# A decoder layer with self-attention, cross-attention and a ternary feed-forward: the projections of cross-attention spread over all units, and all eight key blocks by high and low parts

## The reference

```
x = x + attn(layernorm(x))        # 16 heads of 128, window of 128 keys, rope, sink
x = x + xattn(layernorm(x), ctx)  # below
x = x + ffn(layernorm(x))         # 8-bit rows, ternary weights, Hadamard transform

Q = (query @ Wq).reshape(b, q_len, G, Hpg, dh)       # 512 rows, 16 heads of 32
K = (key @ Wk).reshape(b, kv_len, G, dh)             # 1024 keys, 4 groups of 32
V = (value @ Wv).reshape(b, kv_len, G, dh)
scores = einsum('bqghd,bkgd->bghqk', Q, K) / sqrt(dh) + m * rel
w = softmax(where(mask, scores, neg), axis=-1)
out = einsum('bghqk,bkgd->bqghd', w, V).reshape(b, q_len, G * Hpg * dh) @ Wo
```

## Time and profile before

| | |
|---|---|
| median of three runs | 1842.2 us (1842.17 to 1844.28) |
| profiled execution, its own time | 1846.15 us |
| span from first to last instruction in it | 1844.3 us |
| busy: PE, DVE, ACT, POOL | 1667.3, 1161.6, 1238.9, 1176.8 us |
| mean granted clock of PE | 0.973 |

### The profile page before, as it was taken

How to read it: one execution, slowest core, us unless ns; L and a number is a source line. 1 busy time by engine, 2 the same in 40 slices (tenths; PEclk the granted TensorE clock), 3 DMA queues, 4 the chain that set the end, 5 groups by cost and what they waited for, 6 DMA issues and landing times. The chain is left out here.

```text
span 1844.3 us, 24894 instructions
## 1 busy us (share of the span) xinstructions
PE 1667.3 (90%) x8112; PEld 1164.3 (63%) x8112; DVE 1161.6 (63%) x2031; ACT 1238.9 (67%) x2018; POOL 1176.8 (64%) x1080
## 2 busy tenths in 40 slices
PE   6999979899999957999999999999999966999996
PEld 3588868788888845556655565556555523666664
DVE  2378868677666743666675558655776724677763
ACT  2366768787656631797777678766886924878775
POOL 0477857678778810566665557555675727888892
PEclk9999989999999988999999999999999988999999
DMA  6222343333000012311211122011011211011000
GB/s 218 103 66 85 98 127 109 92 115 127 13 18 7 29 42 67 107 40 36 72 46 49 35 75 61 12 38 44 18 43 41 97 58 64 13 35 35 24 18 23
DMA packets 57647, 110.76 MB, mean 60 GB/s; under 512 B 9132, under 2 KB 13996, under 8 KB 57136
## 3 DMA queue, kind: packets, MB, share of 16 engines
q1 hardware_dynamic: 55680, 108.04, 18.8%
q10 hardware_dynamic: 1840, 1.14, 0.2%
HBM read 71.33 MB, written 18.88 MB: 49 GB/s over the span
## 5 line engine op out<-in xcount | busy, mean ns | idle before, releaser
L1263 POOL TENSOR_TENSOR x_p_lo<-x_p,x_p_hi 128x1024 fp32r<-128x1024 f32 x192 | 455.7, 2385 | 300.6 <-ACT x_p_hi L1097 300.1
L1212 DVE TENSOR_REDUCE x_maxes<-x_ps_a 128x1 f32<-128x1024 f32 x256 | 313.1, 1223 | 258.5 <-PE x_ps_a L1346 257.6
L1075 ACT ACTIVATE x_p<-x_ps_b,x_any_valid 128x1024 f32<-128x1024 f32 x256 | 285.1, 1114 | 168.7 <-PE x_ps_b L1334 167.9
L1334 PE MATMUL x_ps_b<-x_Q,x_K 100*128 100x512 f32 x512 | 228.3, 527 | 3.7 <-ACT x_p L1075 2.2
L1097 ACT ACTIVATE x_p_hi<-x_p 128x1024 fp32r<-128x1024 f32 x192 | 203.1, 1058 | 4.8
L1346 PE MATMUL x_ps_a<-x_K,x_Q 99*128 99x512 f32 x512 | 166.8, 407 | 6.4 <-DMA x_Q<-x_p_lo 3.7
L1372 PE MATMUL x_ps_o<-x_p_hi,x_V 128*96 128x512 f32 x384 | 157.2, 409 | 1.1 <-POOL x_p_lo L1263 1.1
L1334 PEld LDWEIGHTS x_ps_b<-x_Q,x_K 100*128 100x128 f32 x512 | 90.1, 190 | 97.2 <-issue 76.2
L1373 PE MATMUL x_ps_o<-x_p_lo,x_V 128*96 128x512 f32 x384 | 150.9, 393 | 0.0
L427 ACT ACTIVATE a_work<-a_ps_s,a_neg_max,a_q_r 128x256 f32<-128x256 f32 (+1 forms) x256 | 134.1, 540 | 4.6 <-DVE a_neg_max L527 4.6
L619 POOL TENSOR_TENSOR a_work<-a_work,a_inv_den 128x1024 f32<-128x1024 f32 (+1 forms) x64 | 110.0, 1719 | 18.6 <-DVE a_inv_den L567 18.6
(11 more groups left out here) (243 smaller groups left out, 4315.4 us busy)
## 6 DMA issues: line engine op xcount, KB each, us to landing
shared<-in_L_attn_out_w SPq DMA_DIRECT2D x8, 1024.0 KB, 7.7
shared<-in_L_ffn_w_gate SPq DMA_DIRECT2D x16, 512.0 KB, 4.5
shared<-in_L_ffn_w_up SPq DMA_DIRECT2D x16, 512.0 KB, 4.1
shared<-in_L_ffn_w_down SPq DMA_DIRECT2D x16, 512.0 KB, 4.1
shared<-in_ctx SPq DMA_DIRECT2D x8, 1024.0 KB, 7.0
x_Q<-x_q_hi SPq DMA_DIRECT2D x104, 64.0 KB, 2.0
ffn_quant<-shared SPq DMA_DIRECT2D x24, 256.0 KB, 4.6
a_xt<-in_x SPq DMA_DIRECT2D x16, 256.0 KB, 4.9
```

Source lines behind the costliest of these rows:

```text
L1075: act.activation(p[:, r, :, :], ps_b[:, :, :], ACT.Exp, scale=any_valid[:, b % 2:b % 2 + 1]).then_inc(exp_ready, 1)
L1212: dve.tensor_reduce(out=maxes[:, h2, r, 3:4], in_=ps_a[:, :, :], axis=mybir.AxisListType.XY, op=ALU.max)\
L1263: pool.tensor_tensor(out=p_lo[:, r], in0=p[:, r], in1=p_hi[:, r].bitcast(F32), op=ALU.subtract).then_inc(lo_ready, 1)
L1334: last = pe.matmul(ps_b[:, j, :], K[0:ROWS + 4, g, kb * P:(kb + 1) * P], Q[0:ROWS + 4, hh, :], start=True, stop=True)
```

## The change

In cross-attention:

- All four units of a head now go by high and low parts. `V32` and the plain fp32 matmuls are gone, `V` holds all eight key blocks, ACT makes `p_hi` and POOL `p_lo` in every unit. `p` is a ring of three (was four, one to each r), `p_hi` of four (was three), `p_lo` stays at three, each with the waits that belong to it. `aT` has five slots instead of four.
- The jobs are no longer bound to heads. A table `ORDER` of twelve jobs gives job n of a batch the units 5n to 5n + 3, so that every fifth unit has none. Part 2 of Q is now made in the batch that uses it. The transposed norm goes through `ps_x` (units r = 3 of heads 2 to 5), not through `ps_j`.
- The prologue projects keys before it transposes the norm, makes two parts of Q instead of three, and copies the constant key rows later.
- The last output projection runs over the head groups outside and the four tiles inside, into four banks.

In self-attention the rounding of weights moves two steps later, and the exchange of sums is split into `store_sums` (steps 9, 17, 25) and `load_sums` (steps 11, 19, 27). In the feed-forward phase the first two tiles are loaded already during cross-attention, and the constants are waited for later.

```diff
-            def exchange_sums(t):
+            def store_sums(t):
                 sp.wait_ge(f_sum_ready, t + 1)
                 sp.dma_start(ffn_total[t:t + 1, :].rearrange("a p -> p a"), f_sum[:, t:t + 1]).then_inc(f_sum_out, 16)
+
+            def load_sums(t):
                 sp.wait_ge(f_sum_out, 16 * (t + 1))
                 sp.dma_start(f_all[:, t, :], ffn_total[t:t + 1, :].broadcast_to([P, P])).then_inc(f_all_in, 16)
...
-                if 0 <= c - 16 < FFN_CHUNKS:
-                    store_quant(c - 16)
-                if 0 <= c - 12 < FFN_CHUNKS:
-                    load_raw(c - 12)
+                if 0 <= c - 18 < FFN_CHUNKS:
+                    store_quant(c - 18)
+                if 0 <= c - 14 < FFN_CHUNKS:
+                    load_raw(c - 14)
                 if c in (9, 17, 25):
-                    exchange_sums(c // 8 - 1)
+                    store_sums(c // 8 - 1)
+                if c in (11, 19, 27):
+                    load_sums(c // 8 - 1)
...
-        V = sb("V", [P, 2, 6, GX, 3 * DH], F32R)
-        V32 = sb("V32", [P, 2, 2, GX, 3 * DH])
+        V = sb("V", [P, 2, KB, GX, 3 * DH], F32R)
         maxes = sb("maxes", [P, HX, TPB, 4])
-        p = sb("p", [P, 4, 2, T])
-        p_hi = sb("p_hi", [P, 3, 2, T], F32R)
+        p = sb("p", [P, 3, 2, T])
+        p_hi = sb("p_hi", [P, 4, 2, T], F32R)
         p_lo = sb("p_lo", [P, 3, 2, T], F32R)
...
+        ORDER = (("Q", 2, 0), ("Q", 3, 0), ("K", 0, 1), ("K", 1, 1), ("out", 0, -1), ("out", 1, -1), ("out", 2, -1), ("out", 3, -1),
+                 ("Q", 0, 1), ("V", 0, 1), ("V", 1, 1), ("Q", 1, 1))
+        pieces, finished, finished_at = {}, [], {}
+        for b in range(-1, B):
+            jobs = [(8 * b + 4 * (n - 9), (name, i, 0)) for n, (name, i, later) in enumerate(ORDER) if name == "V"] if b < 0 else \
+                [(4 * HX * b + 5 * n, (name, i, b + later)) for n, (name, i, later) in enumerate(ORDER) if 0 <= b + later < B]
...
-                    if c and r < 3:
-                        act.wait_ge(lo_ready, 3 * (c - 1) + r + 1)
-                    if c and r == 3:
-                        act.wait_ge(pv_done, 4 * c)
-                    act.activation(p[:, r, :, :], ps_b[:, :, :], ACT.Exp, scale=any_valid[:, b % 2:b % 2 + 1]).then_inc(exp_ready, 1)
+                    if v >= 3:
+                        act.wait_ge(lo_ready, v - 2)
+                    act.activation(p[:, v % 3, :, :], ps_b[:, :, :], ACT.Exp, scale=any_valid[:, b % 2:b % 2 + 1]).then_inc(exp_ready, 1)
...
-                if 0 <= c < HEADS and r < 3:
-                    pool.wait_ge(hi_ready, 3 * c + r + 1)
-                    if c:
-                        pool.wait_ge(pv_done, v - 3)
-                    pool.tensor_tensor(out=p_lo[:, r], in0=p[:, r], in1=p_hi[:, r].bitcast(F32), op=ALU.subtract).then_inc(lo_ready, 1)
+                if 0 <= c < HEADS:
+                    pool.wait_ge(hi_ready, v + 1)
+                    if v >= 3:
+                        pool.wait_ge(pv_done, v - 2)
+                    else:
+                        pool.wait_ge(q_spread[1], 192)
+                    pool.tensor_tensor(out=p_lo[:, v % 3], in0=p[:, v % 3], in1=p_hi[:, r].bitcast(F32), op=ALU.subtract).then_inc(lo_ready, 1)
...
-                    if rw < 3:
-                        pe.wait_ge(lo_ready, 3 * kw + rw + 1)
-                        for j in range(2):
-                            vs = V[:, bw % 2, 2 * rw + j, gw, :]
-                            pe.matmul(bank[0:ROWS, :], vs, p_hi[:, rw, j], start=(rw == 0 and j == 0), stop=False)
-                            last = pe.matmul(bank[0:ROWS, :], vs, p_lo[:, rw, j], start=False, stop=False)
-                    else:
-                        pe.wait_ge(exp_ready, w + 1)
-                        for j in range(2):
-                            last = pe.matmul(bank[0:ROWS, :], V32[:, bw % 2, j, gw, :], p[:, 3, j], start=False, stop=(j == 1))
+                    pe.wait_ge(lo_ready, w + 1)
+                    for j in range(2):
+                        vs = V[:, bw % 2, 2 * rw + j, gw, :]
+                        pe.matmul(bank[0:ROWS, :], vs, p_hi[:, rw, j], start=(rw == 0 and j == 0), stop=False)
+                        last = pe.matmul(bank[0:ROWS, :], vs, p_lo[:, w % 3, j], start=False, stop=(rw == 3 and j == 1))
...
+            for k in range(GX):
+                G = GX * (B - 1) + k
+                pe.wait_ge(aT_ready, G + 1)
+                for i in range(TPB):
+                    last = pe.matmul(banks[i], aT[:, G % (GX + 1), i * P:(i + 1) * P], wo_sb[:, k, :], start=(k == 0), stop=(k == GX - 1))
+                    if k == GX - 1:
+                        last.then_inc(job_made, 1)
```

260 lines of the change are left out of this document (127 added, 133 removed).

## The result

The kernel after takes 1790.3 us (median of four runs, 1788.45 to 1790.5) against 1842.2 us for the kernel before in the same session: a ratio of 0.971 (95% interval 0.970 to 0.973), faster by 2.9%. The forecast was 1786 us. The profiled execution took 1788.45 us for a span of 1786.2; for it the sum of the prediction gave about 1790.

The account below looks back on a forecast made before the run. PE was taken as the bound, narrowly in free heads. Terms -30 - 14 - 2 - 5 - 5 = -56 us took the profiled 1846.15 us to about 1790; the median, 4 us lower, gave 1786 us, 8-in-10 range 1765 to 1808.

Parts of the forecast that it names:

- Units of cross-attention: Cross-attention stage: two middle batches -14.0 us each, first batch -7, last +4.5; together -30 us, bounds -50 and -10.
- The step on the output projection: First output piece waits for aT behind p_lo; ACT partly catches up, leaving 3 to 3.5 us, three times.
- The step on free units: Around job-free units in cross-attention, late exponentials make PE wait 6 to 7 us a batch, 1.5 more at its end.
- rival 1: Cross-attention: PE stays the bound throughout; batch 176 us, stage -50, whole 1766 us; chance 0.20.
- The plain matmuls go: Cross-attention: replacing plain fp32 matmuls saves PE 0.78 us a head, 12.5 a batch, 50 us over 64 heads.
- the spreading: Cross-attention: with a unit between jobs, PE's hand-over waits at ps_j go, most of 12.2 us in a batch.
- Free heads: Cross-attention heads without a job: bound by POOL and ACT at about 9.76 us, 9.27 before.
- Self-attention: Weight rounding: ACT's waits of 9.8 and 6.4 us for a stored chunk go; -14 us, bounds -18 and 0.
- feed-forward: Start of the feed-forward phase: rows in place, only memsets ahead of layer norm; -5 us, bounds -5 and -1.
- Rival 2: Cross-attention: ACT and POOL hold PE up in every head; stage -8 us, whole 1808 us; chance 0.22.
- rival 4: Cross-attention: VectorE slows p_lo on POOL; at 3.2 us each the kernel takes about 1870 us; chance 0.04.
- Rival 3: Self-attention: the wait only moves, the store landing late instead of being issued late; whole 1800 us; chance 0.09.

Follow-up runs that it names:

- e1: Kernel after, with POOL making aT ahead of p_lo instead of behind it in units r = 3; 1773.5 us.
- e9: Kernel after, with four useless plain fp32 matmuls filling PE's wait for aT at the first piece of the output projection; 1785.6 us.
- e5: Kernel before, with only the high and low parts for all eight key blocks, jobs still bound to heads; 1869.9 us.
- e6: Kernel after, with the last two key blocks of a head in plain fp32 and the old rings, new job order kept; 1787.4 us.
- e7: Kernel after with aT made ahead of p_lo, and ACT's copy into den moved to DVE; 1777.7 us.
- e3: Kernel after, with self-attention's weight rounding and exchange of sums as in the kernel before; 1800.4 us.

## Why the prediction was right, and where it was not

The total was right by 4 us. A part of this is luck. The spans of the two profiled executions differ by 58.1 us (1844.3 to 1786.2) where the sum had 56, but the medians by 51.9: the prediction took 4 us off because the kernel before was profiled in an execution 4 us above its median, and the kernel after was profiled in one 2 us below its own. The parts, by the two spans:

- **Units of cross-attention: -33.9 for -30.** The middle batch was 184.3 for 185.3, the first 9.6 us shorter for 7, the last 15 heads 6.3 longer for 4.5. The agreement in the middle batch is luck: errors that cancel. The step on the output projection, "ACT catches up its own lateness meanwhile, so I count 3 to 3.5 us, three times", failed: the wait itself was sized well (4.04 for 4.4), but it was not made good, and the clock, for which the sum has no term, fell behind it. e1 takes away 5.4 us at each place and leaves a wait of 1.2, e9 puts 2.6 of the 5.4 to the clock. So this place costs 3.4 us more than the 3.2 of the sum, and the low clock of head 46 another 1.6. The step on free units, "6 to 7 us in a batch, with 1.5 us more", was too high by 4: there are 3.3 us of waits for exponentials in a middle batch, 1.7 of them in the four free units at its end and 1.6 in all others. And PE's own work is 172.75 us at the full clock (e1) where the sum had 174.6. Together +3.4, +1.6, -4.2 and -1.9 make the 1 us between forecast and trace. With aT out of the way the batch is 177.2 us, so away from that one place rival 1 (176 us) describes the kernel better than the forecast does.
- **"The plain matmuls go ... 50 us over 64 heads".** The size per head was exact where PE is the bound (13.36 to 12.58), but the term is no gain of its own. Alone it made the kernel 28 us slower (e5); with the jobs spread and aT first it is worth 14 us (e6 against e1). What carried the change is the spreading: 37.6 us over the 63 heads without the high and low parts. The prediction took 12.2 us of waits out of a middle batch and put 10.7 us of new ones in, so that spreading had 1.5 of its 14 us; by e6 it is 13.4 us in that batch (199.0 to 185.6).
- **Free heads: 9.78 for 9.76.** Right; which engine sets it was left as "POOL and ACT". e7 shows ACT first: with one copy less on ACT the head is 9.36 us, all of it POOL's work.
- **Self-attention: -13.3 for -14** in the two profiled spans, but -9.5 to -10 by e3 and the means over all traces. The two spans flatter this term by 3 to 4 us. The step took the waits as nearly gone ("no wait on the stored chunk above 2 us"); waits of 2.8 and 3.4 us are left.
- **Prologue -3.2 for -2, end of cross-attention -4.6 for -5, feed-forward -3.1 for -5.** The first two are sizes: the prologue lasts 38.0 to 38.6 us in the eleven traces with its code. The last failed in its step "only the memsets are ahead": the layer norm does start at once, but POOL's `f_ln_rstd` comes 4.9 us into the phase, and the identity lands 8.5 us after its issue. So the term is not there at all: the 3.1 us are what two traces happen to differ by, and the means over all traces are 0.3 us apart (326.5 and 326.2).
- **Rival 2** (PE held in every head, 7.2 us in units with a piece) is refuted by 3.3 us of waits for exponentials in the whole of a middle batch, **rival 4** by p_lo, which stayed at 2.34 to 2.44 us in all 256. **Rival 3** (the wait in self-attention only moves) holds for less than half: of 16.9 us of waits on the chunk 7.3 are left.

## What to carry to other kernels

Where a change saves work on the bound engine, ask next who hands it its buffers: 0.78 us less a head was worth nothing until the bank's hand-over lay beside other work, and the two edits together were worth more than their sum. Look for the one in-order wait with a whole pipeline behind it, and price it as the wait, less what is shown to be caught up, plus PE's low clock behind it; here three such places cost 16.5 us, more than the 14 us that the high and low parts bring. On an engine that feeds both the steady stream and a rare consumer, put the rare product first where somebody is about to wait for it.
